# Scale factors ahead of the sines, a mean product moved up, and wide GpSimd products behind the last scaling

## What is computed

```
u  = group_norm(x) as tokens                 # 16 x 256 x 96
fx = layer_norm(u) * g1 + b1
lam_bar = exp(lam * exp(log_step))           # 48 complex modes
B_bar   = (lam_bar - 1) / lam * B
xs  = scan over tokens: s = lam_bar * s + B_bar fx
y   = 2 Re(C xs) + D * fx
y   = gelu(y) + fx
fy  = layer_norm(y) * g2 + b2
z1, z2 = split(fy @ W_enc.T)
out = x + (z1 * gelu(z2)) @ W_dec.T + fy
```

## Time and profile before

| | |
|---|---|
| median of 3 runs | 114.44 us (106.93, 114.44, 114.79) |
| the profiled execution | 107.66 us, of which the span of the trace is 105.6 us |
| TensorE busy | 95.9 us (91% of the span), its weight loads 55.7 us |
| VectorE busy | 72.7 us (69%) |
| ScalarE busy | 43.9 us (42%) |
| GpSimd busy | 38.5 us (36%) |
| chain that ended last | PE 48%, DVE 27%, DMA 7%, ACT 6%, issue 4%, POOL 2% |

### The profile page before, as it was taken

One profiled execution on the slowest core, in us unless ns is written; L12 is line 12 of the kernel. 1 busy time (PEld: TensorE's weight loads), 2 busy tenths in 40 slices (PEclk: granted clock), 3 DMA queues, 4 the chain that ended last, 5 costly groups with the idle time before them and its releaser, 6 DMA issues.

```text
span 105.6 us, 1489 instructions
## 1 busy us (share of the span) xinstructions
PE 95.9 (91%) x500; PEld 55.7 (53%) x500; DVE 72.7 (69%) x220; ACT 43.9 (42%) x93; POOL 38.5 (36%) x54
## 2 busy tenths in 40 slices
PE   5999849999979999998999999998799999999960
PEld 3667537755646756765675555675243532533300
DVE  1649992899997698655839312689970499994590
ACT  1309029999739200110094049445079422025200
POOL 7710378600399930000029000028992000395000
PEclk9999999999999999999999999999999999999999
DMA  3999000000000000000000000000000000550125
GB/s 73 263 243 210 17 0 0 0 6 0 3 0 0 0 0 0 6 0 0 0 3 0 0 0 0 6 0 0 0 0 0 0 0 0 141 161 2 43 80 175
DMA packets 3767, 3.79 MB, mean 36 GB/s; under 512 B 496, under 2 KB 3664, under 8 KB 3760
## 3 DMA queue, kind: packets, MB, share of 16 engines
q1 hardware_dynamic: 3392, 3.49, 13.0%
q10 hardware_dynamic: 368, 0.20, 0.7%
HBM read 2.12 MB, written 1.57 MB: 35 GB/s over the span
## 4 chain that ended last, share of the span: by engine, by line
PE 48%; DVE 27%; DMA 7%; ACT 6%; issue 4%; POOL 2%; SPq 1%; DVEq 1%; ACTq 0%
PE ps L491 48%; DMA xs<-x_dram 7%; DVE rs L742 4%; DVE pm L830 4%; DVE rs L772 3%; ACT sq L421 2%; DVE upper L746 2%; ACT xc L423 2%; DVE fy L742 2%; DVE w L742 1%; POOL tb L274 1%; DVE rs L747 1%; ACT y L449 1%; SPq L247 1%; DVE sq L742 1%
## 5 line engine op out<-in xcount | busy, mean ns | idle before, releaser
L341 POOL TENSOR_TENSOR y<-gl,fx 96x512 f32<-96x512 f32 x4 | 6.6, 1662 | 29.8 <-ACT gl L443 29.8
L491 PE MATMUL ps<-fy,mt 96*96 96x512 f32 x32 | 14.9, 600 | 1.3 <-DVE fy L742 1.3
L491 PE MATMUL ps<-wm 96*96 96x256 f32 x46 | 14.3, 468 | 1.2 <-DVE wm L978 1.2
L349 POOL TENSOR_TENSOR res<-fy,xs 96x512 f32<-96x512 f32 x8 | 10.7, 1358 | 11.6 <-DVE fy L742 11.5
L449 ACT ACTIVATE y<-ps,vecs 96x512 f32<-96x512 f32 x8 | 5.5, 686 | 16.5 <-PE ps L491 16.5
L491 PEld LDWEIGHTS ps<-wm 96*96 96x96 f32 x46 | 8.9, 204 | 4.6 <-DVE wm L978 1.2
L491 PE MATMUL ps<-xs,pm 96*96 96x256 f32 x32 | 8.8, 397 | 2.7 <-DVE pm L830 1.8
L742 DVE SCALAR_TENSOR_TENSOR w<-ps,vecs,y 96x512 f32<-96x512 f32 x8 | 6.0, 744 | 7.4 <-ACT y L449 7.4
L491 PEld LDWEIGHTS ps<-fy,mt 96*96 96x96 f32 x32 | 5.0, 163 | 8.7 <-issue 6.9
L491 PE MATMUL ps<-fx,dm 96*96 96x512 f32 x16 | 8.4, 606 | 0.4 <-DVE Z L878 0.4
L878 DVE TENSOR_TENSOR Z<-Z,ps 96x240 f32<-96x240 f32 (+3 forms) x8 | 2.8, 354 | 8.1 <-PE ps L491 8.1
(11 more groups left out here) (120 smaller groups left out, 165.5 us busy)
## 6 DMA issues: line engine op xcount, KB each, us to landing
out_dram<-sq SPq DMA_DIRECT2D x8, 192.0 KB, 2.4
xs<-x_dram SPq DMA_DIRECT2D x3, 384.0 KB, 7.4
xs<-x_dram SPq DMA_DIRECT2D x2, 192.0 KB, 3.6
mt<-mats_dram SPq DMA_DIRECT2D x1, 338.6 KB, 8.0
mt<-mats_dram ACTq DMA_DIRECT2D x1, 180.0 KB, 4.1
sm<-small_dram ACTq DMA_DIRECT2D x1, 8.6 KB, 2.6
cmask<-mask_dram ACTq DMA_DIRECT2D x1, 9.0 KB, 6.2
```

Of the source, the lines that this page charges most:

```text
L341: nc.gpsimd.tensor_tensor(yv[:, RT * i:RT * (i + 1), :], cols(gl, H, i).rearrange("c (b m) -> c b m", b=RT), cols(fx, H, i).rearrange("c ( ...
L349: nc.gpsimd.tensor_tensor(cols(res, H, i), cols(fy, H, i), xs[:, HB * H + 2 * i:HB * H + 2 * i + 2, :].rearrange("c n l -> c (n l)"), ALU. ...
L491: return nc.tensor.matmul(o, lhsT, rhs, start=start, stop=stop)
```

## The change

Five edits in one. ScalarE's two sines go from ahead of its six scalings to behind them. The second half's mean product stands ahead of image 5's centering on TensorE, not of image 6's. The three one-column products for `vecs` stand behind the first variance sums, where a warm-up matmul was; ScalarE copies them ahead of the rotations; TensorE waits for that copy ahead of image 2 of half 1, and one more warm-up matmul goes. GpSimd's wide products wait for VectorE's tenth scaling (`pm_ready`) where they waited for the first inverse root. And the early matrices are loaded from SyncE's queue behind the first half of x.

```
-WARM = (12, 1, 4, 3, 1, 2)
+WARM = (12, 1, 4, 2, 2)
...
                 sp.dma_start(xs[:, first:last, :], x[:, first:last, :]).then_inc(in_x[k], 16)
+                if last == HB:
+                    sp.dma_start(mt[:, 0:N_EARLY], mats[:, 0:N_EARLY]).then_inc(in_early, 16)
...
             pool.wait_ge(in_mats, 16)
-            pool.wait_ge(inv_ready[0], 1)
+            pool.wait_ge(pm_ready, FIRST_PM + HB)
...
-            act.dma_start(mt[:, 0:N_EARLY], mats[:, 0:N_EARLY]).then_inc(in_early, 16)
...
-            act.wait_ge(angles_ready, 1)
-            nc.scalar.activation(tbl(SIN), tbl(RED), ACT.Sin).then_inc(sines_ready, 1)
-            nc.scalar.activation(tbl(SH), tbl(RED), ACT.Sin, scale=0.5).then_inc(sines_ready, 1)
+            def sines():
+
+                act.wait_ge(angles_ready, 1)
+                nc.scalar.activation(tbl(SIN), tbl(RED), ACT.Sin).then_inc(sines_ready, 1)
+                nc.scalar.activation(tbl(SH), tbl(RED), ACT.Sin, scale=0.5).then_inc(sines_ready, 1)
...
             for n in range(FIRST_PM, HB):
                 scale_centering(n)
+            sines()
             group_bias(0)
             squares(0, 0, 2)
             centered_values(0, 0, 2)
             squares(0, 2, HB)
             centered_values(0, 2, HB)
+            act.wait_ge(vecs_done, 1)
+            nc.scalar.activation(vecs[:, :], bank(1, 1)[0:96, 0:3], ACT.Copy).then_inc(vecs_ready, 1)
             rotations()
...
             first_state(0)
-            act.wait_ge(vecs_done, 1)
-            nc.scalar.activation(vecs[:, :], bank(1, 1)[0:96, 0:3], ACT.Copy).then_inc(vecs_ready, 1)
...
-                        if H == 1 and i == 1:
-                            pe.wait_ge(vecs_ready, 1)
...
             for n in range(2, HB):
-                if n == 6:
+                if n == 5:
                     group_mean(1)
                 center_batch(0, n)
...
             for i in range(NT):
                 variances(0, 0, i)
-            warm_up(WARM[4], bank(1, 0))
+            mm(bank(1, 1)[0:96, 0:1], m(M_WE), s(B2))
+            mm(bank(1, 1)[0:96, 1:2], m(M_WE + 96), s(B2))
+            mm(bank(1, 1)[0:96, 2:3], m(M_P), s(B1)).then_inc(vecs_done, 1)
             center_batch(1, 0)
             group_bias(1)
-            for n in range(1, 4):
-                center_batch(1, n)
-            warm_up(WARM[5], bank(1, 2))
+            center_batch(1, 1)
+            pe.wait_ge(vecs_ready, 1)
+            center_batch(1, 2)
+            center_batch(1, 3)
+            warm_up(WARM[4], bank(1, 2))
...
-            pe.wait_ge(taken[0], HB + 4)
-            mm(bank(1, 1)[0:96, 0:1], m(M_WE), s(B2))
-            mm(bank(1, 1)[0:96, 1:2], m(M_WE + 96), s(B2))
-            mm(bank(1, 1)[0:96, 2:3], m(M_P), s(B1)).then_inc(vecs_done, 1)
```

## The result

The changed kernel takes 106.83 us (median of 19 runs, 106.42 to 113.59), the kernel before 108.31 us in 19 runs beside it (106.54 to 114.79). Like runs compared, the ratio is 0.9919, with a 95% interval of 0.9895 to 0.9943: 0.8% or 0.87 us faster, which is within 2%. Both kernels have executions some 7 us longer; comparisons are made of like executions, and the longer ones are told of where the clock is the question. The profiled execution took 106.55 us with a span of 104.6 (before 107.66 and 105.6), at full clock up to the last two microseconds.

The account below looks back on a forecast made before the run. Nearly half the chain of waits was TensorE, with VectorE's four scalings ahead of a long stretch. A 0.6 us gain gave 107.06 from the profiled run and 106.3 from the lowest; forecast between, 106.7, range 105.6 to 114.2.

Parts of the forecast that it names:

- Scalings ahead of the sines: On ScalarE: with the table load now on its path, the bias copy comes 0.35 us earlier, not 2.
- table load at its full price: Rival, chance 0.12: the load costs ScalarE 1.38 us more, nothing of the gain is left, 107.6 us.
- Second mean: On TensorE: the third centering and the variance product come 0.95 us earlier, and VectorE with them.
- GpSimd behind the last scaling: The new wait costs GpSimd nothing (27.8 against 28.03), and TensorE's last centering comes 1.0 us earlier.
- TensorE earlier by 1.45: 1.0 us at the last centering and 0.45 from moved matmuls bring TensorE 1.45 earlier to the second broadcast.
- full gain: Rival, chance 0.18: VectorE's step slips between two GpSimd products and TensorE's 1.45 us count, giving 106.2 us.
- What is late next: At the second broadcast: GpSimd's last product holds VectorE, `parts` comes only 0.2 us earlier, so the gain is 0.6.
- Moved matmuls: On TensorE: three one-column products leave the path at 36.54, making the next product 0.45 us earlier.
- Loads: At VectorE's ninth statistic, which waits for x: nothing taken, with bounds of -0.2 and +0.2 us.
- for the change: Clock rival, chance 0.13: filling TensorE's gap at 13 to 16 removes slow executions; median from 114.44 to 106.7 us.
- against it: Clock rival, chance 0.07: TensorE's stretch from 18.2 gets too thin, the clock falls, costing 7.5 us: 114.6.
- a granted clock under 1.00: Sign named in advance that the forecast is wrong: a granted TensorE clock below 1.00 (2.4 GHz).

Follow-up runs that it names:

- e6: The changed kernel with the second mean product back at its old place ahead of image 6: ratio to the kernel before 0.9919.
- e4: The changed kernel with GpSimd's wait set back to the first inverse root: ratio to the kernel before 0.9896.
- e3: The kernel before with ScalarE's sines alone moved behind its scalings: ratio 0.9921.
- e2: The kernel before with GpSimd's new wait on pm_ready alone: ratio 0.9944.
- e8: The changed kernel with the table load hidden in ScalarE's idle time and GpSimd's seventh wide product late: ratio to the kernel before 0.9825, median 105.65 us.
- e11: e8 with the three one-column products, ScalarE's copy, TensorE's wait and the warm-up matmul back at their old places: ratio to the kernel before 0.9855.
- e12: The changed kernel with the early matrices loaded from ScalarE's queue again: ratio to the kernel before 0.9946.
- the late product: The changed kernel with GpSimd's seventh wide product waiting until the second inverse root is done: ratio to the kernel before 0.9852.
- e10: e8 with a matmul ahead of each of TensorE's two waits for ScalarE's squares near 20: ratio to the kernel before 0.9883.
- e7: The changed kernel with a one-column sine behind the mask's copy, so the table load falls into ScalarE's idle time: ratio to the kernel before 0.9896.

## Why the prediction was right, and which step was not

The forecast was no change beyond 2% and 106.7 us, and both held (0.8% and 106.83). The chain that sets the gain held as well: VectorE's second inverse root is held by GpSimd's products, and the broadcast waits for `parts`. That 106.7 came so near is partly luck. The starting point, 107.3 from the lowest run and the profiled one, lay 0.5 under the median of the ten executions of the kernel before that took under 109 us (107.85), and the gain of 0.6 was 0.2 to 0.3 too small: two misses that offset each other. By its steps:

- **Scalings ahead of the sines.** Held: of the 0.55 us at the bias copy 0.29 is the start of this execution, and 0.26 was gained where I forecast 0.35. The load takes 1.29 us to the next activation, so "table load at its full price" is out. The Trainium skill, "ScalarE: Activation LUTs", What ACT_TABLE_LOAD costs, adds a drain of about 1380 ns; no such idle time stands behind the load here, nor ahead of it (the scalings end at 14.97, the load starts at 14.99).
- **Second mean.** The variance product came 1.08 earlier by the yardstick (0.95 forecast), because the third centering follows the bias product by 0.12 and not 0.22. The mean's own place is worth nothing (e6), as forecast.
- **GpSimd behind the last scaling.** This step failed in its two halves. "The new wait costs it nothing" was counted against the kernel before; against the same kernel without the wait GpSimd starts 0.70 later by the yardstick, its last product ends 0.62 later, and VectorE is held that much longer: 0.63 us (e4). And the 1.0 us at the last centering was put down to the wait, where VectorE's earlier row alone brings it (e3, e4: no idle time there with all four scalings held). In the kernel before, the wait alone does gain 0.6 (e2). The two edits, as I read it, cure the same 0.60 us of idle time, so their gains, 0.9 and 0.6, don't add; e2's own trace, at half clock there, can't show it.
- **TensorE earlier by 1.45.** Held at 1.50 at `dm`. e4, where TensorE is nearly the bound, shows 29.59 - 28.14 = 1.45 at the broadcast: the rival "full gain" is that kernel, not this one.
- **What is late next.** Held: VectorE meets the product before, is held twice, and `parts` comes 0.06 ahead of the broadcast. By the yardstick `parts` is 0.41 earlier and not 0.2: GpSimd started 0.33 earlier and its seven products took 9.91 us instead of 9.99. The broadcast stood 0.47 behind `parts` and now stands 0.06 behind, which is 0.41 more: 0.82 for the 0.6 forecast. The integer step at 35.12 is held too, at 0.85 for 0.23. The Trainium skill, "GPSIMD Engine Reference", Key points, names VectorE instructions in a 2-port mode or with two SBUF inputs. This step has one input, so the row agrees if the step runs in a 2-port mode, which no trace shows.
- **Moved matmuls.** Worth nothing here as I read it, since the wait for `parts` covers them, and 0.35 in e8 (e11).
- **Loads.** Nothing behind the first scaling (28.76 for 28.77 in e12); a gain of 0.2 ahead of it would not be seen.
- **Clock.** I gave "for the change" 0.13 and "against it" 0.07, as rivals to each other. Both occurred, and the sign "a granted clock under 1.00" came in 6 of the changed kernel's 19 executions (four at 0.91, two at 0.97; the others have 0.98 to 1.00). The first is in 23 of 75 executions, but not in most, so the median of the kernel before is 108.31 and not 114.44; three runs had misled there. The second costs about 2 us in some executions, not 7.5. The stretch from 18.2 was busy 6.08 of 7 us, not 5.3, and so much fuller than the one from 12.8 to 15.9, as I had counted; in e6 the clock fell behind it all the same.

## What to carry to other kernels

Price an added wait against the kernel that has all the other edits and not this one: a wait that helps alone can cost its full length once another edit has emptied the place it was for. When several engines are within a microsecond of each other, ask which instruction is held next by a neighbour that now runs at another phase, and look at the trace of each step with a yardstick that leaves out the scatter of the start. A one-column call in an idle stretch takes a table load off ScalarE's path for 0.20 us in that idle stretch, but of the 1.3 us gained there only 0.52 arrived alone, and 0.68 with the late product.

## What the runs showed of the hardware

- In the traces at full clock a float32 or int32 VectorE instruction from SBUF to SBUF that meets one of GpSimd's seven wide products ends 0.06 to 0.15 us behind that product: 0.28 us of work took 1.16 to 1.23, and in e10 0.24 took 1.39. VectorE instructions that read PSUM are not held: a `w` step takes 0.47 us beside the last product (35.90 in the changed kernel) and 0.46 to 0.47 behind it. The four `fx` steps take 2.75 us beside GpSimd's products, and two of them 1.40 at 42.39, where GpSimd is idle.

```profile
28.00 2.75 DVE L744 SCALAR_TENSOR_TENSOR fx<-xc,sm,ps 96x512 f32<-96x512 f32 x4 [0.77 <-PE ps L495]
```

- With the table of the sines in place the scalings, squares and copies need no load of their own: in the changed kernel none stands between 14.99 and 51.69, where the GELU's load comes, and in e7 none between 6.04 and 15.46.
- At the lower clock the row of `rotS` takes 1.80 us in e6 (1.02 in the changed kernel). The 6.8 us of it moved e6's second broadcast to 30.88 by the yardstick, 2.11 behind the changed kernel's, where half of 6.8 would be 3.4: the rest fell into TensorE's waits, as I read it.
